# Two attention phases of a four-layer graph network: turns reordered on four engines, output transposes moved to another PSUM tile, scores issued two tiles at a time

## The chip, the cores and the metric

The kernel runs on one core of a Trainium2 chip. The metric is the device time of one launch in microseconds, the median of several runs. One more execution was taken by the hardware profiler, and all trace rows here come from it.

## The reference, cut to what matters

128 graphs of 64 nodes with 384 features pass through four layers; each adds its result to its input. Layers 0 and 3 are the multi-head attention (12 heads of 32 features) that this change touches:

```python
h = relu(layernorm(x))
# layer 0, B = 128 graphs, N = 64 nodes, D = 384
q, k, v = h @ Wq.T, h @ Wk.T, h @ Wv.T + bv
a = softmax(q @ k.T * D ** -0.5 + adj)     # rows that are all 0 give 0
x = x + (a @ v) @ Wo.T + bo
# layer 3
q, k, v = h @ Wq + bq, h @ Wk + bk, h @ Wv + bv
s = q @ k.T / sqrt(32) + beta * adj        # where adj > 0, else -9e15
x = x + softmax(s) @ v
```

Layers 1 and 2 are graph layers without softmax over heads; the change leaves them as they are.

## The kernel before, in words

The four layers run one after the other as phases l0, l1, l2, l3. `attention_phase` writes l0 (with an output projection, `proj`) and l3 (without). The 8192 rows are cut into 16 groups of 512 rows, a group into 4 tiles of 128 rows (two graphs). One pass over a group is a turn; there are 16 turns in each phase, 0 (opening), 1 to 13 in a hardware loop, 14, and 15 (last). In a turn the engines work on group i (scores, softmax, weighted sum, and in l0 the output projection) and already on group n = i + 1 (transposes of the normalised rows, and queries, keys, values). Every engine executes its queue strictly in the order in which `projected_turn` (l0) or `plain_turn` (l3) issues it; semaphores order the engines among each other. There is no scheduler: the order is written out by hand.

Weight matrices and activations are split in a high and a low part, so `split_matmul` (L52) makes a product of 9 matmuls. The texts use these letters for TensorE's blocks: **Q**, **K** one chunk of queries or keys (9 matmuls of 512 columns, three chunks each in a turn); **V** values of a tile and **P** its output projection (9 of 384 columns); **S** scores of a tile (24 small matmuls, 48 records in the trace, L743); **E** transposes of the exponentials (L750); **W** the weighted sum (L761); **T** transposes of the normalised rows (L722, two tiles make one T here); **O** transposes of the output rows (L769, l0 only). A number is the tile, or for Q and K the chunk.

PSUM has `psS` (4 banks: the scores of one tile and, behind them, the weighted sums), `psP` (2 banks: T and E) and `psW[0]`, `psW[1]` (Q, K, V, P and, before, O). An engine that reads a bank keeps TensorE from writing it; hence waits such as `s_read` (VectorE has read the scores) or `o_set` (VectorE has read the weighted sum and written `o_rows`).

For a tile: VectorE adds the bias to the scores (`add_bias`, L557), reduces the maximum (L562) and in l0 the minimum (`least`, L565); GpSimd subtracts the maximum (`less_maximum`, L284); ScalarE takes the exponential (L375); TensorE transposes it (E), ScalarE copies it (`eT_copy`, L387); W; VectorE divides (`row_output`: L580 `most` and L588 in l0 only, L585, L589). In l0 then O, ScalarE's `oT_hi` (L391), VectorE's `oT_lo` (`oT_parts`, L596), P, ScalarE's `y_copy`, and GpSimd's `result`. VectorE also makes the statistics of group i + 2 (`statistics`, L516 to L522), the low part of the transposed rows (`hT_parts`, L532, `hT_set`) and adds the bias to the values of l0 (`values`, L574, `v_set`).

Of the kernel before, what the change touches and what calls it, by code (L numbers as in the profile page):

```python
# [24 lines left out]
P = 128  # L25
# [63 lines left out]
def attention_phase(nc, ctx, name, shared, x_in, adj_rows, x_out, biases, own_weights, next_weights):  # L89
# [51 lines left out]
    S_end = KC * NODES  # L141
    S_all = psS[:, :, 0:S_end].rearrange("p r (c n) -> p r c n", c=KC)
# [45 lines left out]
    q_bank, k_bank, v_bank = ((0, 1, 1), (0, 0, 0), (1, 0, 1, 1)) if proj else ((0, 0, 0), (1, 1, 1), (0, 1, 0, 1))  # L188
    oT_bank = (1, 1, 1, 0)
# [82 lines left out]
    def _(pool):  # L272
# [29 lines left out]
        def projected_turn(i, opening, ahead, further):  # L302
            less_maximum(i, 0)
            if not opening:
                result(i - 1, 2)
            less_maximum(i, 1)
            if not opening:
                result(i - 1, 3)
            residual(i, 0)
            residual(i, 1)  # L310
            less_maximum(i, 2)
            less_maximum(i, 3)
            if further:
                roots(i + 2)
            residual(i, 2)
            result(i, 0)
            residual(i, 3)
            result(i, 1)
            if not ahead:
                result(i, 2)  # L320
                result(i, 3)

        def plain_turn(i, opening, ahead, further):
# [7 lines left out]
            if further:  # L331
                roots(i + 2)
            residual(i, 2)
            result(i, 1)
# [7 lines left out]
    def _(act):  # L342
# [46 lines left out]
        def oT_parts(i, t):  # L389
            act.wait_ge(oT_done, i * TILES + t + 1)  # L390
            nc.scalar.activation(oT_hi[:, t], psW[oT_bank[t]][:, 0:D].rearrange("p (c n) -> p c n", c=KC), ACT.Copy)\  # L391
              .then_inc(oT_hi_set, 1)
# [10 lines left out]
        def projected_turn(i, opening, ahead, further):  # L403
# [6 lines left out]
            eT_copy(i, 0)  # L410
            if ahead:
                hT_parts(i + 1, 2)
                hT_parts(i + 1, 3)
            exponentials(i, 1)
            if not opening:
                y_copy(i - 1, 3, 0)
            oT_parts(i, 0)
            if ahead:
                queries(i + 1, 0)
            eT_copy(i, 1)  # L420
            exponentials(i, 2)
            if ahead:
                keys(i + 1, 0)
            oT_parts(i, 1)
            eT_copy(i, 2)
            y_copy(i, 0, 0)
            if ahead:
                queries(i + 1, 1)
            exponentials(i, 3)
            oT_parts(i, 2)  # L430
            eT_copy(i, 3)
            if ahead:
                keys(i + 1, 1)
            if further:
                normalise(i + 2, (0, 1))
            if ahead:
                queries(i + 1, 2)
            if further:
                normalise(i + 2, (2, 3))
            if ahead:  # L440
                keys(i + 1, 2)
            oT_parts(i, 3)
            y_copy(i, 1, 1)
# [4 lines left out]
        def plain_turn(i, opening, ahead, further):  # L448
# [5 lines left out]
            eT_copy(i, 0)  # L454
            values(i, 3)
            exponentials(i, 1)
# [3 lines left out]
            eT_copy(i, 1)  # L460
            if ahead:
                keys(i + 1, 0)
            exponentials(i, 2)
            eT_copy(i, 2)
            if ahead:
                keys(i + 1, 1)
            exponentials(i, 3)
# [19 lines left out]
        if proj:  # L487
            queries(0, 0)
            queries(0, 1)
            keys(0, 0)  # L490
            queries(0, 2)
            keys(0, 1)
            keys(0, 2)
        else:
# [7 lines left out]
    def _(dve):  # L502
# [44 lines left out]
        def add_bias(i, t):  # L547
# [7 lines left out]
            dve.wait_ge(s_done, i * TILES + t + 1)  # L555
            bias = bias_qk[:, t:t + 1, :].rearrange("p t (u n) -> p t u n", u=1).broadcast_to([P, HPC, KC, NODES])
            nc.vector.tensor_tensor(s_b[:, t].rearrange("p (c r) n -> p r c n", r=HPC), S_all, bias, ALU.add)\  # L557
# [36 lines left out]
        def oT_parts(i, t):  # L594
            dve.wait_ge(oT_hi_set, i * TILES + t + 1)
            nc.vector.tensor_tensor(oT_lo[:, t], psW[oT_bank[t]][:, 0:D].rearrange("p (c n) -> p c n", c=KC),  # L596
# [22 lines left out]
        if proj:  # L619
            least(0, 0)  # L620
# [3 lines left out]
        def projected_turn(i, opening, ahead, further):  # L624
            step.turn(i, before if ahead else before - 2)
            add_bias(i, 1)
# [4 lines left out]
            add_bias(i, 2)  # L631
            values(i, 3)
            least(i, 1)
            row_output(i, 0)
# [3 lines left out]
            add_bias(i, 3)  # L638
            maximum(i, 2)
            oT_parts(i, 0)  # L640
            maximum(i, 3)
            least(i, 2)
# [4 lines left out]
            row_output(i, 1)  # L647
            oT_parts(i, 1)
            if further:
                shifts(i + 2)  # L650
            least(i, 3)
            row_output(i, 2)
            if ahead:
                values(i + 1, 1)
            oT_parts(i, 2)
            row_output(i, 3)
            if ahead:
                values(i + 1, 2)
                add_bias(i + 1, 0)
                maximum(i + 1, 0)  # L660
            oT_parts(i, 3)
            if ahead:
                least(i + 1, 0)

        def plain_turn(i, opening, ahead, further):
            step.turn(i, before if ahead else before - 2)
            add_bias(i, 1)
# [4 lines left out]
            add_bias(i, 2)  # L672
            maximum(i, 2)
            add_bias(i, 3)
            if ahead:
                hT_parts(i + 1, 2)
                hT_parts(i + 1, 3)
            row_output(i, 0)
            maximum(i, 3)
            if ahead:  # L680
                score_bias(i + 1)
                queries(i + 1, 0)
            if further:
                statistics(i + 2)
            row_output(i, 1)
# [8 lines left out]
            if ahead:  # L694
                add_bias(i + 1, 0)
                maximum(i + 1, 0)

# [3 lines left out]
    def _(pe):  # L701
# [22 lines left out]

        def queries(i, c):
            split_matmul(nc, psW[q_bank[c]][:], w_cols(Q, slice(c * P, (c + 1) * P)), h_cols(slice(0, COLS)))\
                .then_inc(q_done, 1)

        def keys(i, c):
            split_matmul(nc, psW[k_bank[c]][:], w_cols(K, slice(c * P, (c + 1) * P)), h_cols(slice(0, COLS)))\  # L730
                .then_inc(k_done, 1)
# [34 lines left out]
        def out_transposes(i, t):  # L766
            pe.wait_ge(o_set, i * TILES + t + 1)
            for c in range(KC):
                ins = nc.tensor.transpose(psW[oT_bank[t]][:, c * P:(c + 1) * P], o_rows[:, t % 2, c * P:(c + 1) * P],  # L769
# [8 lines left out]
        def projected_turn(i, opening, ahead, further):  # L778
            n = i + 1
            wait_apart(s_read, i * TILES + 1)  # L780
            scores(i, 1)
            if ahead:
                pe.wait_ge(hT_set if opening else eT_set, i * TILES + (TILES if opening else 0))
                transposes(n, 0)
                transposes(n, 1)
            if not opening:
                project(i - 1, 2, 0, transposed=TILES)
            wait_apart(s_read, i * TILES + 2)
            scores(i, 2)
            pe.wait_ge(hT_set if ahead else eT_set, n * TILES + 2 if ahead else i * TILES)  # L790
            exp_transposes(i, 0)
            pe.wait_ge(v_set if opening else y_read, i * TILES + (3 if opening else -2))
            values(i, 3)
            wait_apart(s_read, i * TILES + 3)
            weigh(i, 0)
# [4 lines left out]
            if not opening:  # L800
                pe.wait_ge(y_read, i * TILES - 1)
                project(i - 1, 3, 0)
            wait_apart(o_set, i * TILES + 1)
            scores(i, 3)
            pe.wait_ge(v_set, i * TILES + 4)
            out_transposes(i, 0)
            if ahead:
                if not opening:
                    pe.wait_ge(y_read, i * TILES)
                pe.wait_ge(hT_set, n * TILES + TILES)  # L810
                queries(n, 0)
            else:
                pe.wait_ge(eT_set, i * TILES + 1)
            exp_transposes(i, 1)
            if ahead:
                pe.wait_ge(oT_set, i * TILES + 1)
                values(n, 0)
            wait_apart(s_read, i * TILES + 4)
            weigh(i, 1)
            if ahead:  # L820
                pe.wait_ge(q_set, n * KC + 1)
                keys(n, 0)
                pe.wait_ge(v_set, n * TILES + 1)
            else:
                pe.wait_ge(oT_set, i * TILES + 1)
            out_transposes(i, 1)
            pe.wait_ge(eT_set, i * TILES + 2)
            exp_transposes(i, 2)
# [4 lines left out]
            project(i, 0, 0)  # L833
            if ahead:
                pe.wait_ge(oT_set, i * TILES + 2)
                queries(n, 1)
            wait_apart(o_set, i * TILES + 2)
            weigh(i, 2)
            if ahead:
                pe.wait_ge(y_read, i * TILES + 1)  # L840
                values(n, 1)
                pe.wait_ge(q_set, n * KC + 2)
            else:
                pe.wait_ge(oT_set, i * TILES + 2)
            out_transposes(i, 2)
            pe.wait_ge(eT_set, i * TILES + 3)
            exp_transposes(i, 3)
            if ahead:
                pe.wait_ge(v_set, n * TILES + 2)
                keys(n, 1)  # L850
                pe.wait_ge(oT_set, i * TILES + 3)
                queries(n, 2)
            wait_apart(o_set, i * TILES + 3)
            weigh(i, 3)
            if ahead:
                pe.wait_ge(k_set, n * KC + 2)
                keys(n, 2)
                pe.wait_ge(q_set, n * KC + 3)
                values(n, 2)
# [3 lines left out]
            else:  # L863
                pe.wait_ge(y_read, i * TILES + 1)
            out_transposes(i, 3)
            if ahead:
                pe.wait_ge(v_set, n * TILES + 3)
            project(i, 1, 1)
            if not ahead:
# [4 lines left out]
        def plain_turn(i, opening, ahead, further):  # L874
            n = i + 1
            wait_apart(s_read, i * TILES + 1)
            scores(i, 1)
# [7 lines left out]
            scores(i, 2)  # L885
            pe.wait_ge(hT_set if ahead else eT_set, n * TILES + 2 if ahead else i * TILES)
# [3 lines left out]
            wait_apart(s_read, i * TILES + 3)  # L890
            scores(i, 3)
            if ahead:
                pe.wait_ge(eT_set, i * TILES + 1)
                transposes(n, 2)
                transposes(n, 3)
            wait_apart(s_read, i * TILES + 4)
            weigh(i, 0)
            if ahead:
                pe.wait_ge(v_set, i * TILES + 3)
                pe.wait_ge(hT_set, n * TILES + TILES)  # L900
                queries(n, 0)
            else:
                pe.wait_ge(eT_set, i * TILES + 1)
            exp_transposes(i, 1)
            if ahead:
                pe.wait_ge(v_set, i * TILES + 4)
                keys(n, 0)
# [22 lines left out]
            if ahead:  # L930
# [4 lines left out]
                scores(n, 0)  # L935
                values(n, 1)
# [1504 lines left out]
```

## Time and profile before

| | |
|---|---|
| median of 3 runs | 2984.88 us (2983.04 to 2986.91) |
| the profiled execution: its time, its span | 2989.08 us, 2987.0 us |
| TensorE busy | 2778.8 us, 93% |
| VectorE, ScalarE, GpSimd busy | 1785.4, 1260.3, 1091.1 us |
| middle turns of l0 (14) | 81.22 to 691.41 us |
| middle turns of l3 (14) | 2498.93 to 2960.41 us |

Busy time of TensorE counts modelled ends of pipelined matmuls; the pitch from one block's start to the next tells more than it. A turn is counted from the start of S0 of one group to that of the next.

### The profile page before, as it was taken

How to read it: one execution, taken by the hardware profiler on the slowest of the kernel's cores; microseconds unless marked ns; L12 is line 12 of the kernel's file. 1: busy time of each engine (PE TensorE's matmuls, PEld its weight loads, DVE VectorE, ACT ScalarE, POOL GpSimd, SP SyncE). 2: the span in 40 equal slices, each digit the busy share in tenths (PEclk: the TensorE clock that was granted, in tenths of full speed). 3: DMA queues.
4: the chain of work that ended last, by engine and by line, in shares of the span. 5: the costliest groups of instructions: out<-in, count | busy, mean ns of one | idle time of the engine just before them, and what ended most of it. 6: DMA issues, size and time to landing. Idle time of an engine off the chain costs nothing. (4 is left out here: it accounts for less than half of the span.)

```text
span 2987.0 us, 75491 instructions
## 1 busy us (share of the span) xinstructions
PE 2778.8 (93%) x29312; PEld 2366.3 (79%) x29312; DVE 1785.4 (60%) x4227; ACT 1260.3 (42%) x2212; POOL 1091.1 (37%) x1081
## 2 busy tenths in 40 slices
PE   6999999996899999999986999999999969999998
PEld 5777777775788888888866888888888857777877
DVE  5656665664454455445445777787878755555554
ACT  3444343443444444444423334343433325555554
POOL 1323332333232233323322344444444334444444
PEclk9999999998999999999997999999999989999999
DMA  4211211212321122112103111111111121222221
GB/s 136 63 45 60 61 59 46 67 51 72 104 65 42 53 74 64 41 53 74 49 21 96 38 53 53 47 57 47 58 47 50 34 81 58 78 72 77 84 70 54
DMA packets 186659, 183.15 MB, mean 61 GB/s; under 512 B 79568, under 2 KB 186064, under 8 KB 186576
## 3 DMA queue, kind: packets, MB, share of 16 engines
q1 hardware_dynamic: 186576, 181.99, 19.8%
q8 instruction: 59, 0.97, 0.1%
q14 instruction: 24, 0.20, 0.0%
HBM read 131.61 MB, written 50.33 MB: 61 GB/s over the span
## 5 line engine op out<-in xcount | busy, mean ns | idle before, releaser
L52 PE MATMUL l_psW<-w_hi,l_hT_hi 128*128 128x384 f32 x1920 | 681.6, 355 | 0.1
L52 PE MATMUL l_psW<-w_hi,l_hT_lo 128*128 128x384 f32 x1920 | 647.4, 337 | 0.0
L52 PE MATMUL l_psW<-w_lo,l_hT_hi 128*128 128x384 f32 x1920 | 645.1, 336 | 0.0
L52 PE MATMUL l_psW<-l_hT_hi,w_hi 128*128 128x512 f32 x1152 | 484.4, 420 | 40.3 <-DVE l_hT_lo L532 19.8
L52 PE MATMUL l_psW<-l_hT_hi,w_lo 128*128 128x512 f32 x1152 | 459.9, 399 | 0.0
L52 PE MATMUL l_psW<-l_hT_lo,w_hi 128*128 128x512 f32 x1152 | 458.3, 398 | 0.0
L52 PEld LDWEIGHTS l_psW<-w_hi,l_hT_hi 128*128 128x128 f32 x1920 | 361.8, 188 | 36.1 <-issue 24.6
L52 PEld LDWEIGHTS l_psW<-w_lo,l_hT_hi 128*128 128x128 f32 x1920 | 362.8, 189 | 0.8
L52 PEld LDWEIGHTS l_psW<-w_hi,l_hT_lo 128*128 128x128 f32 x1920 | 361.6, 188 | 0.0
L52 PEld LDWEIGHTS l_psW<-l_hT_hi,w_hi 128*128 128x128 f32 x1152 | 222.3, 193 | 106.4 <-issue 42.0
L284 POOL TENSOR_TENSOR l_s_d<-l_s_b,l_mx 128x768 f32<-128x768 f32 x128 | 188.7, 1474 | 257.8 <-ACT l_e_x L375 144.6
L52 PEld LDWEIGHTS l_psW<-l_hT_hi,w_lo 128*128 128x128 f32 x1152 | 221.4, 192 | 50.3
L52 PEld LDWEIGHTS l_psW<-l_hT_lo,w_hi 128*128 128x128 f32 x1152 | 222.9, 194 | 38.9
L1264 ACT ACTIVATE l_m<-l_psW 128x512 f32<-128x512 f32 x192 | 114.7, 598 | 324.0 <-PE l_psW L52 324.0
L1361 DVE TENSOR_TENSOR l_hT_lo<-l_hT_whole,l_hT_hi 128x512 fp32r<-128x512 f32 x96 | 87.3, 909 | 252.3 <-ACT l_hT_whole L1257 128.7
L295 POOL TENSOR_TENSOR l_xr<-l_xr,l_y_rows 128x384 f32<-128x384 f32 x64 | 64.4, 1006 | 425.4 <-ACT l_y_rows L401 425.4
L1195 POOL TENSOR_TENSOR l_c_root<-l_c_mv,l_half 128x2 f32<-128x2 f32 x64 | 44.7, 698 | 462.2 <-DVE l_c_mv L1392 462.2
L585 DVE RECIPROCAL l_rs<-l_psS 128x12 f32<-128x12 f32 x128 | 29.9, 233 | 243.9 <-PE l_psS L761 243.5
L1836 POOL TENSOR_TENSOR l_right<-l_right,l_b_r 128x384 f32<-128x384 f32 x128 | 132.3, 1037 | 114.6 <-ACT l_right L1914 114.6
L1841 POOL TENSOR_TENSOR l_c_scale<-l_c_var,l_half 128x2 f32<-128x2 f32 x64 | 51.5, 805 | 319.0 <-DVE l_c_var L2064 319.0
L387 ACT ACTIVATE l_eT<-l_psP 128x768 f32<-128x768 f32 x128 | 103.9, 812 | 149.7 <-PE l_psP L750 148.6
L574 DVE TENSOR_TENSOR l_vX<-l_psW,l_bv 64x192 f32<-64x192 f32 x256 | 91.1, 356 | 92.7 <-PE l_psW L52 90.1
(160 smaller groups left out, 5269.5 us busy)
## 6 DMA issues: line engine op xcount, KB each, us to landing
after_l<-l_xr SPq DMA_DIRECT2D x192, 192.0 KB, 1.9
l_xl<-after_l SPq DMA_DIRECT2D x47, 768.0 KB, 4.6
l_xr<-after_l SPq DMA_DIRECT2D x32, 768.0 KB, 4.5
l_xl<-in_x SPq DMA_DIRECT2D x16, 768.0 KB, 5.3
l_xr<-in_x SPq DMA_DIRECT2D x64, 192.0 KB, 2.4
l_xr<-after_l SPq DMA_DIRECT2D x64, 192.0 KB, 2.3
out_x<-l_xr SPq DMA_DIRECT2D x64, 192.0 KB, 1.9
l_adj<-in_adj SPq DMA_DIRECT2D x48, 128.0 KB, 2.3
```

What stands on the lines that cost most here:

```text
L52: last = nc.tensor.matmul(out, lhs[a](c), rhs[b](c), start=(m == 0), stop=(m == n - 1))
L284: nc.gpsimd.tensor_tensor(s_d[:], s_b[:, t], mx[:, t, :].rearrange("p (h n) -> p h n", n=1).broadcast_to([P, HEADS, NODES]), ALU.subtract) ...
L295: nc.gpsimd.tensor_tensor(xr[:, t, :], xr[:, t, :], y_rows[:, t % 2, :], ALU.add).then_inc(y_set, 1)
L387: nc.scalar.activation(eT[:, :, :].rearrange("p a n -> p (a n)"), P_all, ACT.Copy).then_inc(eT_set, 1)
L574: ins = nc.vector.tensor_tensor(vX[part, t, g, :, 0:HD], src[:, :, b, :], bias, ALU.add)
L585: step.done(nc.vector.reciprocal(sums, O_all[:, :, :, HD]))
L1195: nc.gpsimd.tensor_tensor(c_root[:, pair], c_mv[:, pair, 1], half[:, 1:2].broadcast_to([P, PAIR]), ALU.pow)\
L1264: nc.scalar.activation(m[:, j // KC, j % KC, :], psW[j % 2][:], ACT.Copy).then_inc(m_set, 1)
L1361: nc.vector.tensor_tensor(hT[b][1][:, c, :], hT_whole[b][:, c, :], hT[b][0][:, c, :].bitcast(F32), ALU.subtract)\
L1836: nc.gpsimd.tensor_tensor(right[:, t, :], right[:, t, :], b_r[:, u.layer, :], ALU.add).then_inc(right_set, 1)
L1841: nc.gpsimd.tensor_tensor(c_scale[:, pair], c_var[:, pair], half[:].broadcast_to([P, PAIR]), ALU.pow)\
```

## The change

It rewrites the order of the two attention phases on TensorE, VectorE, ScalarE and GpSimd.

- `psS` holds the scores of two tiles (S_end doubles). S of tiles 0 and 1 are issued in one burst at the end of the turn before, S of tiles 2 and 3 in one burst within the turn. `add_bias` of either tile waits for both.
- In l0 the output transposes O go to `psP` (bank t % 2) and no longer to `psW`; the banks of Q, K, V are dealt out anew, V2 of l0 moves to the next turn's start.
- In l3 the first chunk of queries and keys is issued in halves of 256 columns; the first halves need only tiles 0 and 1 of the transposed rows.
- In l0 VectorE makes `row_output(1)` ahead of the statistics, and takes the minima later.

```diff
-    S_end = KC * NODES
+    S_cols = KC * NODES
+    S_end = 2 * S_cols
-    q_bank, k_bank, v_bank = ((0, 1, 1), (0, 0, 0), (1, 0, 1, 1)) if proj else ...
-    oT_bank = (1, 1, 1, 0)
+    q_bank, k_bank, v_bank = ((1, 1, 0), (0, 0, 1), (1, 1, 1, 1)) if proj else ...
...
-            dve.wait_ge(s_done, i * TILES + t + 1)
+            dve.wait_ge(s_done, i * TILES + (t | 1) + 1)
...
# VectorE, projected_turn
-            least(i, 2)
-            if further:
-                statistics(i + 2)
-            if ahead:
-                values(i + 1, 0)
-            row_output(i, 1)
+            maximum(i, 3)
+            least(i, 1)
+            oT_parts(i, 0)
+            row_output(i, 1)
+            if further:
+                statistics(i + 2)
+            if ahead:
+                values(i + 1, 0)
+            oT_parts(i, 1)
...
# TensorE, projected_turn
+            wait_apart(o_set, i * TILES + 2)
+            weigh(i, 2)
             out_transposes(i, 1)
...
             project(i, 0, 0)
+            pe.wait_ge(oT_set, i * TILES + 2)
+            exp_transposes(i, 3)
...
                 wait_apart(k_set, n * KC + 3)
                 scores(n, 0)
+                scores(n, 1)
+                values(n, 2)
...
# TensorE, plain_turn
+                pe.wait_ge(v_set, i * TILES + 3)
+                product(psW[q_bank[0]], Q, 0, first_half)
             wait_apart(s_read, i * TILES + 4)
             weigh(i, 0)
             if ahead:
-                pe.wait_ge(hT_set, n * TILES + TILES)
-                queries(n, 0)
+                pe.wait_ge(v_set, i * TILES + 4)
+                product(psW[k_bank[0]], K, 0, first_half)
+            pe.wait_ge(hT_set if ahead else eT_set, n * TILES + TILES if ahead else i * TILES + 1)
             exp_transposes(i, 1)
             if ahead:
-                keys(n, 0)
+                product(psW[q_bank[0]], Q, 0, second_half).then_inc(q_done, 1)
+                product(psW[k_bank[0]], K, 0, second_half).then_inc(k_done, 1)
```

TensorE in the loop turn of l0, at the second output transposes. Before, the last matmuls of K0, O1 into `psW1`, E2, and P0:

```order
L52 MATMUL l0_psW0<-l0_hT_hi,w_hi 128x512
L52 MATMUL l0_psW0<-l0_hT_lo,w_hi 128x512
L52 MATMUL l0_psW0<-l0_hT_hi,w_lo 128x512
L769 MATMUL l0_psW1<-ident,l0_o_rows 128x128 x3
L750 MATMUL l0_psP<-ident,l0_e_x 128x128 x6
L52 MATMUL l0_psW0<-w_hi,l0_oT_hi 128x384
```

In the changed kernel the same transposes O1, now after V0 of the next group and W2, and into `psP`:

```order
L52 MATMUL l0_psW1<-w_hi,l0_hT_hi 128x384
L52 MATMUL l0_psW1<-w_lo,l0_hT_hi 128x384
L52 MATMUL l0_psW1<-w_hi,l0_hT_lo 128x384
L761 MATMUL l0_psS<-l0_vX,l0_eT 64x33 x24
L769 MATMUL l0_psP<-ident,l0_o_rows 128x128 x3
L52 MATMUL l0_psW0<-w_hi,l0_oT_hi 128x384
```

O1 stood right behind K0; now E2, V0 and W2 stand between K0 and it, and P0 follows it.

VectorE in the loop turn of l0, around the statistics. Before: minimum, statistics (BN rows), values V0, then `row_output(1)` from `most` on:

```order
L565 TENSOR_REDUCE l0_mn<-l0_s_b 128x12
L514 ISA
L516 BN_STATS l0_stats<-l0_xl 128x6 x4
L70 REGISTER_ALU
L518 MEMSET l0_pause 128x1
L520 BN_AGGR l0_mv<-l0_stats 128x2 x4
L70 REGISTER_ALU
L522 TENSOR_SCALAR l0_var<-l0_mv 128x4
L574 TENSOR_TENSOR l0_vX<-l0_psW1,l0_bv 64x6x32 x4
L580 SCALAR_TENSOR_TENSOR l0_most<-l0_mn,l0_mx 128x12
L585 RECIPROCAL l0_rs<-l0_psS 128x4x3
```

In the changed kernel `oT_lo` of tile 0 and `row_output(1)` come first:

```order
L595 TENSOR_TENSOR l0_oT_lo<-l0_psP,l0_oT_hi 128x384
L579 SCALAR_TENSOR_TENSOR l0_most<-l0_mn,l0_mx 128x12
L584 RECIPROCAL l0_rs<-l0_psS 128x4x3
L70 REGISTER_ALU
L587 SCALAR_TENSOR_TENSOR l0_rs<-l0_most,l0_rs 128x12
L70 REGISTER_ALU
L588 TENSOR_TENSOR l0_o_rows<-l0_psS,l0_rs 128x4x3x32
L513 ISA
L515 BN_STATS l0_stats<-l0_xl 128x6 x4
```

The statistics and V0's bias addition moved from ahead of `row_output(1)` to behind it; `oT_parts(1)` now stands behind both.

TensorE in the loop turn of l3, before W0. Before: S3, T of tiles 2 and 3, W0, and then Q0 at its full width:

```order
L743 MATMUL l3_psS<-l3_kT,l3_qT 64x64 x24
L720 REGISTER_ALU
L722 MATMUL l3_psP<-ident,l3_h 128x128 x3
L720 REGISTER_ALU
L722 MATMUL l3_psP<-ident,l3_h 128x128 x3
L709 REGISTER_ALU
L761 MATMUL l3_psS<-l3_vX,l3_eT 64x33 x24
L52 MATMUL l3_psW0<-l3_hT_hi,w_hi 128x512
```

In the changed kernel the second T tile's successor is a half of Q0 (its last matmuls are shown), and a half of K0 follows W0:

```order
L52 MATMUL l3_psW0<-l3_hT_hi,w_hi 128x256
L52 MATMUL l3_psW0<-l3_hT_lo,w_hi 128x256
L52 MATMUL l3_psW0<-l3_hT_hi,w_lo 128x256
L707 REGISTER_ALU
L761 MATMUL l3_psS<-l3_vX,l3_eT 64x33 x24
L52 MATMUL l3_psW1<-l3_hT_hi,w_hi 128x256
```

A product that waits for all four tiles stood behind W0; now half products that need two tiles stand on both sides of it.

## Rows read from the trace of the kernel before

**Rows 1.** Windows: start:end, length, busy (x instructions) by engine, granted clock, DMA

```profile
81.22:691.41 610.19, 557.62 (x7814) 477.54 (x7813) 381.89 (x871) 247.07 (x416) 204.66 (x181) 0.97 0.19 56
257.33:299.78 42.45, 38.57 (x560) 32.87 (x559) 27.46 (x63) 17.82 (x30) 14.69 (x13) 1.00 0.19 59
299.78:343.85 44.07, 40.20 (x560) 34.49 (x559) 27.45 (x63) 17.82 (x30) 14.69 (x13) 0.96 0.20 57
2498.93:2960.41 461.48, 439.95 (x7142) 366.72 (x7141) 253.44 (x493) 246.97 (x486) 204.94 (x182) 0.97 0.24 75
2631.47:2663.41 31.94, 30.40 (x512) 25.45 (x511) 18.23 (x36) 17.81 (x35) 14.71 (x14) 1.00 0.26 78
```

**Rows 2.** Waits of TensorE, 14 middle turns of l0, then of l3

```profile
PE l_psW L769 <- DVE l_o_rows L589: 26.0, 14, 2.0
...
PE l_psW L52 <- DVE l_hT_lo L532: 17.4, 14, 1.2
```

**Rows 3.** Timeline of TensorE in l0: start, length, line, operation, idle before

```profile
301.41 0.44 PE L52 MATMUL l_psW<-w_hi,l_oT_hi 128*128 128x384 f32 x1 [0.37 <-DVE l_vX L574]
...
303.16 0.78 PE L743 MATMUL l_psS<-l_kT,l_qT 32*64 32x64 f32 x48
303.87 0.88 PE L722 MATMUL l_psP<-ident,l_h 128*128 128x128 f32 x6
304.50 0.42 PE L52 MATMUL l_psW<-w_hi,l_oT_hi 128*128 128x384 f32 x1
...
307.42 0.85 PE L750 MATMUL l_psP<-ident,l_e_x 128*128 128x128 f32 x6 [0.39 <-ACT l_e_x L375]
308.02 0.42 PE L52 MATMUL l_psW<-w_hi,l_hT_hi 128*128 128x384 f32 x1
...
321.88 0.39 PE L52 MATMUL l_psW<-l_hT_hi,w_lo 128*128 128x512 f32 x1
324.24 0.87 PE L769 MATMUL l_psW<-ident,l_o_rows 128*128 128x128 f32 x3 [1.97 <-DVE l_o_rows L589]
...
328.43 0.39 PE L52 MATMUL l_psW<-l_hT_hi,w_hi 128*128 128x512 f32 x1
...
330.59 0.90 PE L761 MATMUL l_psS<-l_vX,l_eT 64*64 64x33 f32 x48
331.42 0.44 PE L52 MATMUL l_psW<-w_hi,l_hT_hi 128*128 128x384 f32 x1
```

**Rows 4.** Timeline of VectorE and GpSimd in l0, the same turn

```profile
301.38 0.96 DVE L557 TENSOR_TENSOR l_s_b<-l_psS,l_adj 128x768 f32<-128x768 f32 x1
302.37 0.95 DVE L562 TENSOR_REDUCE l_mx<-l_s_b 128x12 f32<-128x768 f32 x1
...
318.41 1.93 DVE L516 BATCH_NORM_STATS2 l_stats<-l_xl 128x6 f32<-128x384 f32 x4
...
320.87 1.46 DVE L574 TENSOR_TENSOR l_vX<-l_psW,l_bv 64x192 f32<-64x192 f32 x4
322.36 0.69 DVE L580 SCALAR_TENSOR_TENSOR l_most<-l_mn,l_mx 128x12 f32<-128x12 f32 x1
...
323.54 0.56 DVE L589 TENSOR_TENSOR l_o_rows<-l_psS,l_rs 128x384 f32<-128x384 f32 x1
...
327.08 0.16 DVE L580 SCALAR_TENSOR_TENSOR l_most<-l_mn,l_mx 128x12 f32<-128x12 f32 x1
...
322.03 1.00 POOL L290 TENSOR_TENSOR l_xr<-l_xr,l_bo 128x384 f32<-128x384 f32 x1
```

**Rows 5.** Timeline of l3 at the wait for the low parts: TensorE, then VectorE

```profile
2709.60 0.47 PE L52 MATMUL l_psW<-l_hT_hi,w_hi 128*128 128x512 f32 x1 [1.25 <-DVE l_hT_lo L532]
...
2708.43 1.02 DVE L532 TENSOR_TENSOR l_hT_lo<-l_psP,l_hT_hi 128x384 fp32r<-128x384 f32 x2 [1.08 <-ACT l_hT_hi L358]
```

**Rows 6.** Groups of TensorE by form, whole span: busy us, mean ns of one

```profile
L52 PE MATMUL l_psW<-w_hi,l_hT_lo 128*128 128x384 f32 x1920 | 647.4, 337 | 0.0
...
L52 PE MATMUL l_psW<-l_hT_lo,w_hi 128*128 128x512 f32 x1152 | 458.3, 398 | 0.0
```

More of the change, by code:

```diff
@@ L306, in projected_turn @@
             less_maximum(i, 1)
+            residual(i, 0)
             if not opening:
                 result(i - 1, 3)
-            residual(i, 0)
+            less_maximum(i, 2)
             residual(i, 1)
-            less_maximum(i, 2)
             less_maximum(i, 3)
@@ L315, in projected_turn @@
             residual(i, 2)
+            residual(i, 3)
             result(i, 0)
-            residual(i, 3)
             result(i, 1)
@@ L390, in oT_parts @@
             act.wait_ge(oT_done, i * TILES + t + 1)
-            nc.scalar.activation(oT_hi[:, t], psW[oT_bank[t]][:, 0:D].rearrange("p (c n) -> p c n", c=KC), ACT.Copy)\
+            nc.scalar.activation(oT_hi[:, t], psP[:, t % 2, 0:D].rearrange("p (c n) -> p c n", c=KC), ACT.Copy)\
               .then_inc(oT_hi_set, 1)
@@ L436, in projected_turn @@
             if ahead:
-                queries(i + 1, 2)
+                keys(i + 1, 1)
+            oT_parts(i, 3)
             if further:
@@ L440, in projected_turn @@
             if ahead:
+                queries(i + 1, 2)
                 keys(i + 1, 2)
-            oT_parts(i, 3)
-            y_copy(i, 1, 1)
+            y_copy(i, 1, 0 if ahead else 1)
             if not ahead:
@@ L625, in projected_turn @@
             step.turn(i, before if ahead else before - 2)
-            add_bias(i, 1)
+            if not opening:
+                values(i, 2)
             if ahead:
@@ L637, in projected_turn @@
                 hT_parts(i + 1, 3)
-            add_bias(i, 3)
+            least(i, 0)
+            row_output(i, 0)
             maximum(i, 2)
+            maximum(i, 3)
+            least(i, 1)
             oT_parts(i, 0)
-            maximum(i, 3)
-            least(i, 2)
+            row_output(i, 1)
             if further:
@@ L646, in projected_turn @@
                 values(i + 1, 0)
-            row_output(i, 1)
             oT_parts(i, 1)
+            least(i, 2)
+            row_output(i, 2)
             if further:
@@ L677, in plain_turn @@
                 hT_parts(i + 1, 3)
+            maximum(i, 3)
             row_output(i, 0)
-            maximum(i, 3)
             if ahead:
@@ L862, in projected_turn @@
                 scores(n, 0)
+                scores(n, 1)
+                values(n, 2)
             else:
+                project(i, 1, 1)
                 pe.wait_ge(y_read, i * TILES + 1)
[L865 to L869, printed above, removed]
                 project(i, 2, 0, transposed=TILES)
```

181 lines of the change are left out of this document (78 added, 103 removed).

## The prediction

> **What bounds the kernel now.** I read the windows of whole turns first. The 14 middle turns of l0 take 610.19 us, 43.59 each, those of l3 461.48 us, 32.96 each [rows 1]. TensorE is busy 38.57 us of a 42.45 us turn of l0 and 30.40 of a 31.94 us turn of l3, VectorE only 27.46 and 18.23: TensorE's queue is the bound in both phases, and what can be won is its idle time, 3.88 and 1.54 us a turn, not another engine's.
>
> A second loss stands beside it. The turn from 299.78 has the same instructions as the one before it but takes 44.07 us at a mean granted clock of 0.96 instead of 42.45 us at 1.00 [rows 1]: one stretch at the lower of the clock's two levels (1.2 instead of 2.4 GHz) costs 1.62 us. It comes behind the longest idle time: from 324.24, after 1.97 us in which TensorE did nothing, until the block at 328.43, O1, E2 and P0 take 4.19 us instead of the 2.65 that their pitches below add up to [rows 3]. The mean turn of 43.59 lies near the slower kind, so most turns pay it. In l3 the mean of 32.96 against 31.94 at full clock says the same.
>
> The list of waits names the causes. In l0 the largest is O1 for `o_rows`, 26.0 us in 14 turns; in l3 it is Q0 for `hT_lo`, 17.4 us in 14 [rows 2]. The timeline of VectorE shows why the first is late: from 318.41 it makes the statistics, then V0's addition at 320.87, and only at 322.36 turns to `row_output(1)`, whose last instruction ends at 323.54 + 0.56 = 324.10; TensorE starts O1 at 324.24 [rows 4, 3]. In l3 two `hT_lo` instructions begin at 2708.43 and end at 2709.45, and Q0 starts at 2709.60 [rows 5].
>
> **Prices of the blocks.** By pitch, start to start [rows 3]: P or V 1.75 (301.41 to 303.16), S 0.71, T 0.63, E 0.60, W 0.83, Q or K 2.16 (328.43 to 330.59), O half of E, 0.30 (half as many transposes).
>
> **l0, what is removed.** No arithmetic goes away, so a turn without any wait is the 42.45 us turn less its gaps. The idle of 3.88 us is counted from modelled ends: the last matmul of K0 starts at 321.88, its successor would start 2.16 / 9 = 0.24 later, at 322.12, so the gap before 324.24 is 2.12 where the view says 1.97. Five such gaps in a turn (E0, S3, O1, K1, P1) hide about 0.8 more. 42.45 - 3.88 - 0.8 = 37.8 us.
>
> **l0, what is added.** I laid out the new order by these pitches from the burst S0, S1 on.
> The burst ends at 1.42; VectorE's first addition starts about 0.2 later and the second, after addition and maximum (0.99 and 0.87 apart, rows 4), ends near 4.4. TensorE has V2, T and P2 (4.1 us) before S2, S3, which start at 5.5: covered. Behind the burst, E0 would start at 6.9; `hT_lo` of tiles 0 and 1 comes behind V2's addition (1.5) and ends about 6.9 too: covered with nothing to spare, take 0 to 0.3.
> O1 now has E2, V0 and W2 ahead of it: its `row_output` no longer waits for the statistics and is over 0.8 us before W2 wants it.
> The stall moves to what stands behind the statistics, `oT_parts(1)`, for which E3 waits, since O1 fills `psP`. From O0 on TensorE has O0, K0, E2, V0, W2, O1, P0 = 0.30 + 2.16 + 0.60 + 1.75 + 0.83 + 0.30 + 1.75 = 7.7 us until E3. VectorE has in the same time: waiting for `oT_hi` (about 1.1) and `oT_lo` (0.5), `row_output(1)`, the statistics (318.41 to 320.87, 2.46), V0's addition (1.50) and `oT_lo` (0.56), 6.1 without `row_output`. That one takes 1.1 when nothing disturbs it (7.2 in all, no wait) and more when GpSimd works: `most` took 0.69 instead of 0.16 us and ended at 323.05, just when GpSimd's instruction begun at 322.03 ended at 323.03 [rows 4]. In the new order GpSimd is in `residual(1)` and `less_maximum(3)` at this place, so I take 2.3 for it: 8.4, and a wait of 0.7 to 0.8 at E3. If it is undisturbed the wait is nothing; if it is hit by two whole instructions of GpSimd, 2.3.
> A rule of the Trainium skill speaks of this: "SBUF — State Buffer", section "SBUF: two separate sides", says that a VectorE instruction with two SBUF inputs and a GpSimd instruction shut each other out for the whole instruction. By that rule both L580 and L588 are exposed in each `row_output`; the trace agrees for L580 (0.69 us).
> So a turn of l0 takes 37.8 + 0.8 = 38.6 us, with no idle time near 1.97 us left, and I expect no stretch at the low clock. Gain 14 x (43.59 - 38.6) = 69.9 us.
>
> **l3.** The 1.54 us idle (1.8 by pitch: two gaps, 0.15 each hidden) go: from T on TensorE has Q0's first half, W0, K0's first half (about 3.2 us) before it needs `hT_lo` of tiles 2 and 3, where before only W0's 0.83 covered it and 1.25 were missing.
> The halves are the price. No matmul of 256 columns stands in the trace. By form one of 512 columns has 398 ns and one of 384 has 337 [rows 6], 61 ns for 128 columns; a block of 9 falls from 1.75 to 1.75 - 0.55 = 1.20, two halves cost 2.40 against 2.16, at most 0.24 for each of two products. Part of a pitch is the fixed start of a block, and the second halves stand back to back; I take 0.3 a turn for both. Bounds: 0, and 2 x (2 x 1.75 - 2.16) = 2.7 if 256 columns cost what 384 do.
> The Trainium skill ("TensorE: Matmul & The Clock Gate", "Back-to-back issue gap" and "LDWEIGHTS") gives N / 2.4 + 2.5 ns for a matmul and P / 1.2 for its weights, so 109 and 107 ns at 256 columns: the weights would stay just hidden and the sum would be an estimated 0.05 us a turn instead of 0.3. No run here shows that width yet.
> The pair bursts of l3 are covered as in l0 (V1, T, V2 = 4.1 us against the additions' 4.4 - 1.4).
> A turn takes 31.94 - 1.8 + 0.3 = 30.4 us; gain 14 x (32.96 - 30.4) = 35.8 us.
>
> **The end turns.** I give l0's opening nothing (V1 and V2 now follow S0, S1 and VectorE must add their bias before the first score bias), l0's last a turn's gain (5.0), l3's two ends 2.6 each: 10.2. Bounds 0 and 16.
>
> **Not on the path.** GpSimd, ScalarE and the DMA queue keep their work; with 38.6 us a turn VectorE would be 71% busy.
>
> **Sum.** 69.9 + 35.8 + 10.2 = 116 us. The profiled execution has a span of 2987.0 and a time of 2989.08; the changed one would have 2873. The median of the runs lies 4.2 below the profiled time, which gives 2869.
>
> **Rivals.**
> *The stretch at the low clock stays*, once a turn in both phases, although the long waits are gone: bursts S, S, E are 2.0 us of small matmuls in a row, where before at most S and E stood together. It costs 1.62 x 29 = 47 us: 2916. Against it: in the turn shown only the idle time of 1.97 us was followed by the low clock, none of the shorter ones. Chance 0.08.
> *VectorE becomes the second bound*: its queue has the extra stops above, E0 and E3 wait 0.3 and 2.3 us instead of 0 and 0.8, which is 1.8 x 14 = 25 us more: 2894. Against it: at 40.4 us a turn it would be busy 27.46, 68%. Chance 0.14.
> *Slower than before*: the bursts of small matmuls hold the clock low in place after place (S0 S1; S2 S3 E0; each W with its O). 116 us are eaten at 72 stretches of 1.62 us, more than two a turn in 32 turns; at three a turn, 96, the time is 2869 + 156 = 3025. The fall shown [rows 3] stands behind an idle time, and the new order has none of its length. Chance 0.04.
> *No change*: the waits come back elsewhere to the same sum, 2985. It needs 5 us a turn in l0 of which my layout finds 0.8. Chance 0.02.
> *Forecast*, 2850 to 2890: 0.72.
>
> **How the numbers follow.** Low end: no wait at E3 (-11), halves free (-4), ends at 16 (-6): 2848, say 2850. High end: the halves at the price of 384 columns, 2.4 x 15 = 36 more, 2905, which takes in the second rival as well. About 0.86 of the chance lies within. A measurement of this kernel can tell about 0.2% (6 us) from no change: faster 0.94, same 0.02, slower 0.04.
>
> **What would show it.** Middle turns of 38.6 us in l0 and 30.4 in l3; granted clock 1.00 in both; no wait of L769 for `o_rows`, none of L52 for `hT_lo` in l3; one wait of E (L750) for `oT_lo` near 0.8 us in l0; L579 or L587 longer than 0.16 us; blocks of 256 columns of 1.1 to 1.2 us. Wrong would be: a clock of 0.96 again, E0 waiting over 0.5 us, or blocks near 1.75 us.

## Result, and the profile after

The changed kernel takes 2839.99 us (median of 4 runs, 2837.55 to 2840.32), the kernel before beside it 2984.78 us. The ratio is 0.9513, 95% interval 0.9496 to 0.9529: 145 us less. The forecast was 2869 us with a range of 2850 to 2905: the direction held, the gain was 29 us larger than said, and the time lies 10 us below the range.

The page of the changed kernel, its span and its busy row (us, share of the span, x instructions):

```profile
span 2838.6 us, 75948 instructions
PE 2708.2 (95%) x29582; PEld 2345.1 (83%) x29582; DVE 1802.0 (63%) x4227; ACT 1256.7 (44%) x2212; POOL 1093.8 (39%) x1081
```

The windows of it that answer to [rows 1]: the 14 middle turns of l0, one of them, the 14 middle turns of l3, one of them:

```profile
81.84:604.28 522.44, 518.39 (x7814) 457.00 (x7813) 389.27 (x871) 247.15 (x416) 206.72 (x181) 1.00 0.22 66
305.76:343.10 37.34, 37.06 (x560) 32.67 (x559) 27.97 (x63) 17.82 (x30) 14.84 (x13) 1.00 0.21 67
2399.43:2815.12 415.69, 415.69 (x7394) 369.37 (x7392) 259.81 (x493) 243.63 (x486) 205.55 (x182) 1.00 0.27 82
2577.66:2607.34 29.68, 29.68 (x529) 26.38 (x528) 18.77 (x36) 17.57 (x35) 14.73 (x14) 1.00 0.27 84
```

A middle turn of l0 takes 522.44 / 14 = 37.32 us where it took 43.59, one of l3 29.69 where it took 32.96, and the granted clock, 0.97 before, is 1.00 in both. In l3 TensorE is busy without a break (415.69 of 415.69 us). Its waits in the middle turns (to [rows 2]; total us, times, longest us) are one line in l0 and none in l3:

```profile
PE l_psP L750 <- DVE l_hT_lo L531: 4.1, 14, 0.3
```

The 148.4 us of span (2987.0 to 2838.6) go to: l0's middle turns 610.19 - 522.44 = 87.8, l3's 461.48 - 415.69 = 45.8, and the rest, 14.8, to the end turns and about 1 us to l1 and l2, which have the same code. From l1's first transposes to l3's first it is 2441.37 - 747.19 = 1694.2 before and 2346.67 - 653.51 = 1693.2 after.

### The profile page after: what moved, and what is told of

It reads as the page before. It is cut to its first block and busy times, and to the rows that moved or that the text cites. A ratio compares the mean times of both kernels' runs of the same rounds, so it can differ in the third digit from the quotient of the medians.

```text
span 2838.6 us, 75948 instructions
## 1 busy us (share of the span) xinstructions
PE 2708.2 (95%) x29582; PEld 2345.1 (83%) x29582; DVE 1802.0 (63%) x4227; ACT 1256.7 (44%) x2212; POOL 1093.8 (39%) x1081
## 5 line engine op out<-in xcount | busy, mean ns | idle before, releaser
L52 PE MATMUL l_psW<-w_hi,l_hT_hi 128*128 128x384 f32 x1920 | 681.7, 355 | 2.0 <-DVE l_vX L573 2.0
L52 PE MATMUL l_psW<-w_hi,l_hT_lo 128*128 128x384 f32 x1920 | 647.6, 337 | 0.0
L52 PE MATMUL l_psW<-w_lo,l_hT_hi 128*128 128x384 f32 x1920 | 645.2, 336 | 0.0
L52 PE MATMUL l_psW<-l_hT_hi,w_hi 128*128 128x512 f32 (+1 forms) x1242 | 495.7, 399 | 12.1 <-ACT l_m L1252 3.7
L52 PE MATMUL l_psW<-l_hT_hi,w_lo 128*128 128x512 f32 (+1 forms) x1242 | 469.8, 378 | 0.0
L52 PE MATMUL l_psW<-l_hT_lo,w_hi 128*128 128x512 f32 (+1 forms) x1242 | 469.1, 378 | 0.0
L52 PEld LDWEIGHTS l_psW<-w_hi,l_hT_hi 128*128 128x128 f32 x1920 | 362.0, 189 | 38.5 <-issue 24.6
L52 PEld LDWEIGHTS l_psW<-w_lo,l_hT_hi 128*128 128x128 f32 x1920 | 362.6, 189 | 0.7
L52 PEld LDWEIGHTS l_psW<-w_hi,l_hT_lo 128*128 128x128 f32 x1920 | 361.4, 188 | 0.0
L52 PEld LDWEIGHTS l_psW<-l_hT_hi,w_hi 128*128 128x128 f32 x1242 | 236.0, 190 | 69.6 <-issue 22.1
L52 PEld LDWEIGHTS l_psW<-l_hT_hi,w_lo 128*128 128x128 f32 x1242 | 235.5, 190 | 44.8
L52 PEld LDWEIGHTS l_psW<-l_hT_lo,w_hi 128*128 128x128 f32 x1242 | 236.8, 191 | 35.3
L761 PEld LDWEIGHTS l_psS<-l_vX,l_eT 64*64 64x64 f32 x6144 | 103.1, 136 | 41.0 <-issue 37.1
```

What stands on the lines that cost most here:

```text
L52: last = nc.tensor.matmul(out, lhs[a](c), rhs[b](c), start=(m == 0), stop=(m == n - 1))
L761: ins = nc.tensor.matmul(psS[NODES * g:NODES * (g + 1), r, S_end + c * (HD + 1):S_end + (c + 1) * (HD + 1)], eT[keys_b, a, NODES * g:NODES ...
```

## Where the blocks got cheaper

The pitches of TensorE's blocks (the time from one block's start to the next one's) explain most of what the forecast missed. The timeline of the changed kernel in l0, around the bursts and E0 (start, length; the rows between them left out):

```profile
305.76 1.28 PE L743 MATMUL l_psS<-l_kT,l_qT 32*64 32x64 f32 x96
306.97 0.45 PE L52 MATMUL l_psW<-w_hi,l_hT_hi 128*128 128x384 f32 x1
...
310.98 1.28 PE L743 MATMUL l_psS<-l_kT,l_qT 32*64 32x64 f32 x96
312.54 0.87 PE L750 MATMUL l_psP<-ident,l_e_x 128*128 128x128 f32 x6 [0.28 <-DVE l_hT_lo L531]
```

The pair S0, S1 takes 306.97 - 305.76 = 1.21 us; two single ones took 2 x 0.71 [rows 3]. I summed the pitches of every block of one turn at full clock, from start to start, without the waits, in both traces:

| us a turn | l0 before | l0 after | l3 before | l3 after |
|---|---|---|---|---|
| S (4) | 2.83 | 2.42 | 2.84 | 2.42 |
| V and P (8; 4 in l3) | 13.86 | 13.52 | 7.08 | 6.86 |
| T (2) | 1.26 | 1.14 | 1.26 | 1.14 |
| O (4) | 1.25 | 1.16 | | |
| E (4) | 2.31 | 2.40 | 2.34 | 2.36 |
| W (4) | 3.33 | 3.34 | 3.34 | 3.34 |
| Q and K (6) | 12.98 | 13.01 | 13.23 | 13.56 |
| sum | 37.82 | 36.99 | 30.09 | 29.68 |

The work is the same, yet a turn's blocks are 0.83 us shorter in l0, and in l3 0.41 shorter although the halves add 0.33. A block costs what its neighbours make it cost. The same pitches come back in all 14 middle turns, and the kernel before has most of them too:

- V or P took 1.74 to 1.77 us when S or W followed and anything but Q or K stood ahead. It took 1.65 to 1.70 when T, O, E, Q or K followed, or when Q or K stood ahead, and 1.59 with Q or K ahead and O behind (V1 of the changed kernel).
- T took 0.63 behind S or W and 0.57 behind V; E took 0.60 to 0.63 behind S or W and 0.57 behind Q, K or P.
- W took 0.83 everywhere.

In the new order T stands behind V2 and V3 where it stood behind S or W, and four of the eight V and P of l0 have T, O or E behind them where two had O or Q.

## Experiments

In the diffs, lines are of the changed kernel unless "before" is said. All ratios are to the kernel before, run beside each experiment; microseconds more or less than the changed kernel are against its 2839.99 us. Run again beside c1_split_pair and c2_early_scores it took 2840.13 us (below).

### The statistics ahead of row_output(1)

```diff
             oT_parts(i, 0)
-            row_output(i, 1)
             if further:
                 statistics(i + 2)
+            row_output(i, 1)
             if ahead:
                 values(i + 1, 0)
```

> The changed kernel, but in l0 VectorE makes the statistics ahead of row_output(1), with V0's addition behind it. The statistics take 2.46 us, so row_output(1) would end near 326.9 in the turn from 305.76, and W2, which starts at 326.52, waits 0.4 to 1.0 us. Theory (the clock falls only behind a long idle time): no fall, turns 0.4 to 1.2 us longer, 2846 to 2857 us at clock 1.00. Rival (small-matmul stretches hold the clock low once there is any wait): another 1.6 us a turn, near 2875.

Measured 2845.78 us, ratio 0.9531 [0.9517, 0.9546]. The middle turns take 528.24 / 14 = 37.73 us, 0.41 more, at clock 1.00; the list of waits has W (L761) waiting up to 0.4 us a turn. This short wait cost what it is, and nothing on top; the rival, near 2875 us, fell.

### The old order on VectorE

```diff
             oT_parts(i, 0)
-            row_output(i, 1)
             if further:
                 statistics(i + 2)
             if ahead:
                 values(i + 1, 0)
+            row_output(i, 1)
             oT_parts(i, 1)
```

> The changed kernel with the old order on VectorE in l0: statistics, V0's addition, then row_output(1). V0 ends on TensorE near 326.5, its addition near 328.2, row_output(1) near 329.4, so W2 waits about 2.9 us where it started at 326.52. Theory (the low clock follows an idle time of about 2 us): the turn grows by 2.9 + 1.6, in all 14 x 4.5 = 63 us, near 2903, clock 0.96 in l0. Rival (what lowered the clock before was the mixture of blocks, not the idle time): 14 x 2.9 = 41, near 2881, clock 1.00.

Measured 2926.39 us, ratio 0.9801 [0.9786, 0.9816]: 86 us more, and worse than either theory. The window of its 14 middle turns:

```profile
86.41:690.57 604.16, 552.40 (x7814) 489.34 (x7813) 394.97 (x871) 247.13 (x416) 205.91 (x181) 0.94 0.19 57
```

A turn takes 43.15, 5.8 more: 3.5 us waiting at W2 (2.9 expected), and about 2.3 at the lower clock, more than one stretch of 1.6 a turn (its full turns take 42.4 to 43.9). So the order on VectorE is worth nearly all of l0's gain: with it alone undone, 43.15 of the old 43.59 us are back.

### The new order on VectorE in the kernel before

Two kernels, each the one before with one edit:

```diff
# b1_before_rows_values_stats
-            if further:
-                statistics(i + 2)
+            row_output(i, 1)
             if ahead:
                 values(i + 1, 0)
-            row_output(i, 1)
+            if further:
+                statistics(i + 2)
             oT_parts(i, 1)
# b2_before_rows_stats_values
+            row_output(i, 1)
             if further:
                 statistics(i + 2)
             if ahead:
                 values(i + 1, 0)
-            row_output(i, 1)
             oT_parts(i, 1)
```

> The kernel before, with one edit: in l0 VectorE makes row_output(1), then V0's addition, then the statistics. W1 stands at 319.12 in the turn from 299.78, so o_rows would be there near 320.9 and V0's addition near 322.4; O1, which needs both (its bank is V0's), starts about 0.3 us late instead of 2.1. oT_lo of tile 1 then comes behind the statistics and Q1 may wait 0.4. Theory: the idle time goes and the low clock of l0 with it, 14 x (43.6 - 41.0) = 36 us less, near 2950. Rival (the order on VectorE is not what made O1 late): 2985.

> The kernel before, with the changed kernel's order on VectorE alone: row_output(1), statistics, V0's addition. O1 still writes the bank that V0's addition reads, and that addition would end near 324.9, so O1 waits 2.8 us instead of 2.1. Theory: it gains nothing without O in the other banks; 14 x 0.7 = 10 us more, near 2995, clock as before. Rival: o_rows alone held O1, then near 2950 as in the run beside it.

The first took 2960.69 us, ratio 0.9909 [0.9892, 0.9925]; its middle turns 583.56 / 14 = 41.68 us at clock 1.00. The second took 3011.29 us, ratio 1.0078 [1.0061, 1.0094]; 632.20 / 14 = 45.16 us, at clock 0.95. What its O1 waits for (waits of TensorE, 100 to 600 us, of the second):

```profile
PE l_psW L769 <- DVE l_vX L574: 33.4, 11, 3.0
```

It is no longer `o_rows` but V0's bias addition: O1 writes the bank that VectorE still reads. So the order that helps the changed kernel makes the kernel before slower; it pays only in the changed kernel, where O goes to `psP` and TensorE has its new order (the two were not tried apart). The first kernel shows that a third of l0's gain (1.9 of 6.3 us a turn) was to be had without moving a bank; it is 0.7 above the 41.0 us expected, with O1 still waiting 0.6 us for V0's addition and a product (L52) 0.4 us for `oT_lo`.

### Whole Q0 and K0 in l3

```diff
             if ahead:
                 pe.wait_ge(eT_set, i * TILES + 1)
                 transposes(n, 2)
                 transposes(n, 3)
-                pe.wait_ge(v_set, i * TILES + 3)
-                product(psW[q_bank[0]], Q, 0, first_half)
             wait_apart(s_read, i * TILES + 4)
             weigh(i, 0)
             if ahead:
-                pe.wait_ge(v_set, i * TILES + 4)
-                product(psW[k_bank[0]], K, 0, first_half)
+                pe.wait_ge(v_set, i * TILES + 3)
+                pe.wait_ge(hT_set, n * TILES + TILES)
+                queries(n, 0)
...
             exp_transposes(i, 1)
             if ahead:
-                product(psW[q_bank[0]], Q, 0, second_half).then_inc(q_done, 1)
-                product(psW[k_bank[0]], K, 0, second_half).then_inc(k_done, 1)
+                pe.wait_ge(v_set, i * TILES + 4)
+                keys(n, 0)
```

> The changed kernel with the whole Q0 behind W0 and the whole K0 behind E1 in l3, as before the change, and everything else left. In the turn from 2577.66 hT_lo of tiles 2 and 3 ends at 2589.74 and W0 at 2587.80, so Q0 waits 2.1 us; the halves' price of 0.3 us goes away. Theory: 1.8 us a turn more, and the clock falls again in two of three turns or in all, 1.1 to 1.6 more: 15 x 2.9 to 3.4 = 44 to 51 us, near 2887. Rival (the halves save nothing, the pair bursts do the work in l3): 2840 or below.

Measured 2876.92 us, ratio 0.9637 [0.9622, 0.9651]: 37 us more than the changed kernel. Its waits of TensorE in 14 middle turns of l3, and the place in one turn:

```profile
PE l_psW L52 <- DVE l_hT_lo L531: 26.6, 14, 1.9
```

```profile
2444.16 0.90 PE L761 MATMUL l_psS<-l_vX,l_eT 64*64 64x33 f32 x48
2446.96 0.47 PE L52 MATMUL l_psW<-l_hT_hi,w_hi 128*128 128x512 f32 x1 [1.89 <-DVE l_hT_lo L531]
```

A turn takes 450.24 / 14 = 32.16 us. The 2.47 more are the wait of 2.0 by pitch, less 0.3 for the halves, and 0.7 of the lower clock: of the 14 turns 6 take 33.1 us and 8 take 31.5. The halves are what removes l3's wait; with everything else in place and whole products l3 gains 0.8 us a turn. The rival fell. T, which has W0 behind it here (2443.42 to 2444.16), takes 0.75 us as the median of the 14 turns, where it takes 0.57 with a half product behind it.

The page's groups by form give the price of 256 columns, which the trace before did not have:

```profile
L52 PE MATMUL l_psW<-l_hT_lo,w_hi 128*128 128x256 f32 x180 | 50.7, 282 | 0.0
```

and a half block has a pitch of 1.15 to 1.25 us. The four halves of a turn take 4.72 us where two whole blocks take 4.42 (2.18 and 2.24 for the other chunks): 0.30, the value forecast. The Trainium skill's figures ("TensorE: Matmul & The Clock Gate", "Back-to-back issue gap") led to an estimated 0.05; the runs have the larger one. Within a half block the matmuls stand 0.119 us apart, within a whole one 0.2275, which makes 36 x 0.119 - 18 x 0.2275 = 0.19 us; the rest, 0.11, lies at the starts and ends of the blocks, of which there are four instead of two.

### A met wait within the pair, and a pair taken apart

```diff
# b3_wait_in_pair, both phases, and likewise between scores(n, 0) and scores(n, 1)
             scores(i, 2)
+            wait_apart(s_read, i * TILES + 2)
             scores(i, 3)
# c1_split_pair, l3 only
             scores(i, 2)
-            scores(i, 3)
             pe.wait_ge(hT_set if ahead else eT_set, n * TILES + 2 if ahead else i * TILES)
             exp_transposes(i, 0)
+            scores(i, 3)
```

> The changed kernel with a wait that is already met, of the same kind as the one ahead of the burst, between the two score blocks of each pair in both phases. In the changed kernel a pair takes 1.21 us by pitch where two single blocks took 1.42, 0.21 less, twice a turn. Theory A (each single block paid for the wait ahead of it): about 0.1 to 0.2 us a pair come back, 62 pairs, 6 to 12 us, 2846 to 2852. Theory B (each paid for the change of weight shape, not for the wait): 2840 as the changed kernel.

> The changed kernel, but in l3 S2 and S3 no longer stand together: S2, E0, S3. In the changed kernel a pair of score blocks takes 1.21 us by pitch where two single ones took 1.42, and a met wait between the two gave back only 0.04. Theory (a single block pays where the tile shape of the weights changes, and a pair pays once): two more changes of shape in a turn, 0.2 us a turn, 15 turns, 3 us, 2843; turns of l3 of 29.9 instead of 29.69. Rival (the pair was cheaper for another reason, such as back-to-back banks): turns of 29.69. If the second additions of VectorE come late, E0 or W0 would show a wait, and the pitch of S decides.

With the met wait a pair takes 1.25 us instead of 1.21, and l0's middle turns 523.24 / 14 = 37.37 instead of 37.32: 0.05 a turn for two waits. Its 2845.76 us (ratio 0.9526 [0.951, 0.9542]) are 5.8 more than the changed kernel, though (the intervals of the ratios overlap), and of the 5.2 us by which its span is longer the middle turns give about 1.5. Another 2.2 lie in l0's last turn (51.4 us up to l1's first transposes instead of 49.2) and 1.7 in l1 and l2, whose code is the same; why is open. Theory A is refuted for the turn.

With the pair apart the time is 2849.78 us, ratio 0.9544 [0.9529, 0.9558], and the turn 30.30 us:

```profile
2556.05 0.78 PE L743 MATMUL l_psS<-l_kT,l_qT 32*64 32x64 f32 x48
2557.04 0.85 PE L750 MATMUL l_psP<-ident,l_e_x 128*128 128x128 f32 x6 [0.21 <-ACT l_e_x L375]
2557.82 0.78 PE L743 MATMUL l_psS<-l_kT,l_qT 32*64 32x64 f32 x48
```

The turn grew by 0.61 us, three times the 0.2 expected. A new wait of 0.21 us stands at E0, because the exponentials are not there yet. Without it, S2, E0, S3 take 0.78 + 0.78 + 0.71 = 2.27 us where S2, S3, E0 took 1.21 + 0.64 = 1.85: 0.42 for two more changes of operand shape. Of these, 0.07 can be wait that the view does not show, since a single score block elsewhere takes 0.71. Then 0.21 is on the score blocks, which is just the pair's gain, and 0.14 on E0, which takes 0.78 with a score block behind it and 0.63 or 0.64 with V. The met wait was 0.04: the gain comes from the neighbours. That it is the shape of the operands that counts, and not, say, the PSUM bank written, fits the pitches above but was not tested apart.

### GpSimd beside row_output(1)

```diff
             less_maximum(i, 2)
             residual(i, 1)
+            residual(i, 2)
             less_maximum(i, 3)
             if further:
                 roots(i + 2)
-            residual(i, 2)
             residual(i, 3)
```

> The changed kernel, but in l0 GpSimd makes residual(2) between residual(1) and less_maximum(3), so that it works all through row_output(1) on VectorE. In the changed kernel residual(1) ended at 323.25 and less_maximum(3) began at 323.67, and row_output(1) ran through the gap in 1.02 us. Theory (the prediction's term): L587 is stretched by 0.3 to 0.6 us, the statistics and oT_lo of tile 1 slip by as much, and as ScalarE's oT_hi was 0.22 and E3's start 0.28 later than needed, E3 waits 0 to 0.2: 2840 to 2843. Rival (both small instructions are hit by whole ones, 1.5 us and more): E3 waits 1 us, 2854.

Measured 2861.06 us, ratio 0.9577 [0.9561, 0.9593]: the rival, 7 us above its 2854. First the changed kernel, VectorE's `row_output(1)`, then GpSimd at the same time:

```profile
323.30 0.16 DVE L579 SCALAR_TENSOR_TENSOR l_most<-l_mn,l_mx 128x12 f32<-128x12 f32 x1
...
323.64 0.17 DVE L587 SCALAR_TENSOR_TENSOR l_rs<-l_most,l_rs 128x12 f32<-128x12 f32 x1
...
322.23 1.02 POOL L290 TENSOR_TENSOR l_xr<-l_xr,l_bo 128x384 f32<-128x384 f32 x1
323.67 1.49 POOL L284 TENSOR_TENSOR l_s_d<-l_s_b,l_mx 128x768 f32<-128x768 f32 x1 [0.42 <-ACT l_e_x L375]
```

L579 starts 0.05 us after GpSimd's `residual` has ended (323.25) and L587 0.03 us before its next instruction begins. In the experiment GpSimd goes on without a gap:

```profile
332.64 0.94 DVE L579 SCALAR_TENSOR_TENSOR l_most<-l_mn,l_mx 128x12 f32<-128x12 f32 x1
...
333.76 1.25 DVE L587 SCALAR_TENSOR_TENSOR l_rs<-l_most,l_rs 128x12 f32<-128x12 f32 x1
...
331.57 1.99 POOL L290 TENSOR_TENSOR l_xr<-l_xr,l_bo 128x384 f32<-128x384 f32 x2
333.52 1.47 POOL L284 TENSOR_TENSOR l_s_d<-l_s_b,l_mx 128x768 f32<-128x768 f32 x1
```

Both small instructions end where GpSimd's end (333.58 against 333.56, 335.01 against 334.99). From L579 to the statistics behind it `row_output(1)` takes 2.89 us instead of 1.02, and E3 waits:

```profile
340.09 0.88 PE L750 MATMUL l_psP<-ident,l_e_x 128*128 128x128 f32 x6 [1.29 <-DVE l_oT_lo L595]
```

A turn takes 38.86 us, 1.5 more. The place of one `residual` in GpSimd's queue is worth about 20 us.

### Two improvements

```diff
# a1_low_parts_first, VectorE, l0's turn
-            if not opening:
-                values(i, 2)
             if ahead:
                 hT_parts(i + 1, 0)
                 hT_parts(i + 1, 1)
+            if not opening:
+                values(i, 2)
# c2_early_scores: that, and VectorE ahead of l0's first turn
-            for t in range(TILES - 1):
-                values(0, t)
+            values(0, 0)
...
         add_bias(0, 1)
+        if proj:
+            values(0, 1)
+            values(0, 2)
```

> The changed kernel, but in l0 VectorE makes hT_lo of tiles 0 and 1 ahead of V2's bias addition. In the changed kernel E0 waits 0.28 us in each of the 14 middle turns for hT_lo (0.35 by pitch). Theory: E0 stands behind VectorE's queue, and hT_hi is there (ScalarE done at 310.06) when the second score addition ends (309.99), so the swap removes the wait and V3 still gets its bank: turns of l0 of 37.0 instead of 37.3 us, about 2835 us. Rival: the wait moves to V3, which needs V2's addition; then 2840 as the changed kernel.

> The kernel of a1_low_parts_first, and ahead of l0's first turn VectorE adds the score biases of tiles 0 and 1 before the bias of V1 and V2. In the changed kernel the opening turn of l0 takes 45.2 us, with TensorE waiting 3.8 us before S2 for the score additions and 2.0 us for V1's and V2's. Theory: V1 and V2 no longer stand ahead of the score additions, S2 starts about 3 us earlier, 2832 us. Rival: V2 on TensorE now waits for V1's addition behind the scores, and the time only moves, 2834.6 as the kernel it is made from.

The first took 2834.59 us, ratio 0.9495 [0.9482, 0.9508]: the wait at E0 is gone and TensorE is busy all through its middle turns, 517.91 / 14 = 36.99 us each (the window shown ends within the last block, 0.65 us before the turns do):

```profile
80.84:598.10 517.26, 517.26 (x7810) 456.98 (x7810) 385.23 (x871) 247.11 (x416) 206.71 (x181) 1.00 0.22 66
```

The second took 2830.96 us, ratio 0.9478 [0.9465, 0.9491]; S2 of l0's opening turn starts at 45.03 us where the changed kernel had 48.04. It has the lowest time here, but its lead over the first, 3.6 us, is 0.13%, and the intervals of their ratios overlap. Its opening turn is 3.8 us shorter than the first's (40.5 against 44.3); l0's last turn, and l1 and l2, give 3.2 of that back in the trace.

### The changed kernel again

> The changed kernel once more, beside the others on one chip: 2840 us, turns of 37.3 and 29.7 us; its end turns, where TensorE waits for single results, show how much they vary from run to run (l0's last turn took 49.2 us up to l1's first transposes in the first profile).

2840.13 us, ratio 0.9513 [0.9498, 0.9527]; the middle turns are those of the first profile. From S0 of l0's last turn to l1's first transposes it took 652.58 - 603.66 = 48.9 us, 49.2 in the first profile, and 648.02 - 598.75 = 49.3 in the kernel of a1_low_parts_first, but 51.4 in b3_wait_in_pair and 51.0 in c2_early_scores: the last turn, where TensorE waits for single results, varies between kernels by 2.5 us. From l1's first transposes to l3's first, the same code in all, it varies by 2 us (1692.9 to 1694.9). Differences of a few microseconds between the kernels here can come from there.

## Why the prediction was right, and where it fell short

*The bound, right.* TensorE's queue was the bound, and most of the gain came from its idle time and its clock, as read from [rows 1] and [rows 2]; the rest came from cheaper blocks, of which the prediction had none.

*The stretch at the low clock, right.* It is gone from the middle turns of both phases (0.97 to 1.00). The rival in which bursts of small matmuls hold it low fell: three blocks in a row, S2, S3, E0, leave it at 1.00 in the middle turns of every kernel that has no long idle time. a2 (0.4 us idle, clock 1.00) and a3 (3.5 us, 0.94) bracket it. The rival's premise that "at most S and E stood together" before was misread: W0 and a T stood together for 1.46 us (267.35 to 268.81), against 1.31 of S and E.

*"A turn without any wait is the 42.45 us turn less its gaps ... 37.8", the step that failed.* It took the pitches of the old neighbours for the new order. The sum itself was right for the old order (37.82 in the table), but the blocks of the new order sum to 36.99; the two pairs give 0.41, the rest is V, P, T and O standing beside other blocks than before. The trace before had the warning: in the turn from 257.33 the V at 298.10 had a pitch of 1.68 and the V at 274.92 one of 1.76, and the prediction gave all of them 1.75. The same step in l3, whose gap (1.85 measured, 1.8 said) and halves (0.3) were right, left out 0.7: 29.69 instead of 30.4. Together 14 x (0.83 + 0.76) = 22 of the 32 us of span that were missed. c1 shows the mechanism for the pair by taking one apart; for T and E one neighbour each was changed in a4 and c1 (0.18 and 0.14 us); for V, P and O it rests on the pitches of the two traces.

*"A wait of 0.7 to 0.8 at E3", not there; the second step that failed.* The mechanism is real, b4 has it with a turn of 38.86 us. In the changed kernel `row_output(1)` took 1.02 us, because it fell into GpSimd's gap of 0.42 us; the undisturbed value, which the text gave as the other end. That is 11 us. The prediction had GpSimd at work all through `row_output(1)` and took 2.3 for it; b4, where GpSimd is, measured 2.89.

*"0 to 0.3" at E0, of which I took nothing.* 0.28 us by the view, 0.35 by pitch: 5 us the other way, and a1 took them back.

*The end turns.* 13.8 us where 10.2 was said. l0's opening gave nothing, as said: its S0 came 4.3 us earlier and the turn took 45.21 instead of 40.27, with V1 and V2 behind S0, S1. l0's last turn gave 6.6 instead of 5.0, and l3 the rest.

*The range.* Its low end added the wait at E3, the halves and the ends, but held the block prices fixed, so the one term that moved most had no bounds.

## What to carry to other kernels

When blocks are reordered on TensorE, price them by the pair of neighbours, not by the block: in these traces blocks of equal shape next to each other cost less, and an edit that groups them gained even where no wait was. A reordering on one engine is worth what the banks allow: the same order on VectorE is worth 86 us with the new banks and TensorE's new order, and costs 23 us without them. Before moving work on GpSimd, look what small SBUF-to-SBUF instructions VectorE has at that moment, and after a good result look how narrow the gap was through which they passed.

## What was not expected of the hardware

- Whether the clock falls is not a matter of the idle time alone. With 1.25 us idle at Q0 and 0.3 at W0 just ahead of it, 9 of the 14 middle turns of l3 of the kernel before took the longer time (33.5 against 31.96 us); with 1.89 us at nearly the same place (a4) only 6 of 14 did. What else decides stays open.
- A wait that is already met, on a pair of score blocks, costs TensorE 0.04 us (1.25 against 1.21). A score block apart from the other costs 0.21 us more than in a pair (2 x 0.71 against 1.21).
- L579 and L587, twelve elements a partition, took up to 0.94 and 1.25 us beside GpSimd, while L561 (a reduction over 768 elements) took its 0.94 us beside it too (from 312.33 in the changed kernel, GpSimd at work from 312.07 to 313.07). By the Trainium skill ("SBUF — State Buffer", "SBUF: two separate sides") a VectorE instruction with two SBUF inputs and a GpSimd instruction that reads SBUF keep each other out for the whole instruction; a reduction has one input. The trace agrees for both: L579 and L587 end 0.02 us behind GpSimd's instructions, and L561 is not stretched.
